# Batches 14 and 15 of a transformer layer: the second normalisation in two ScalarE passes, and a new order of the last units

## The reference

```python
x = L0_attn_x                                            # [16, 256, 256] float32
x = x + attn(_layernorm(x), wq, wk, wv, wo)              # 16 heads, 4 KV heads, head size 128
x = x + ffn(_layernorm(x), weight, bias)

# attn: softmax(q k^T / sqrt(128)) v, then wo; a query sees the first 4 keys and the last 32
# ffn:
x_scale = max(max(abs(x), axis=2) / 127, 1e-12)          # one per row
x_q = clip(round(x / x_scale), -128, 127)
y = (x_q @ w_q.T) * x_scale * w_scale + bias             # w_q, w_scale: weight quantised by row
```

## Time and profile before

| | |
|---|---|
| median of three runs | 606.9 us (606.56 to 607.15) |
| the profiled execution: its time | 609.35 us |
| its span, first to last instruction | 607.5 us |
| busy: TensorE, weight load, VectorE, ScalarE, POOL | 593.1, 524.7, 537.0, 397.6, 313.7 us |
| mean granted matmul clock | 0.99 |

### The profile page before, as it was taken

One profiled execution on the slowest core, in us unless ns is written; L12 is line 12 of the kernel. 1 busy time (PEld: TensorE's weight loads), 2 busy tenths in 40 slices (PEclk: granted clock), 3 DMA queues, 4 the chain that ended last, 5 costly groups with the idle time before them and its releaser, 6 DMA issues.

```text
span 607.5 us, 18044 instructions
## 1 busy us (share of the span) xinstructions
PE 593.1 (98%) x7556; PEld 524.7 (86%) x7556; DVE 537.0 (88%) x1073; ACT 397.6 (65%) x625; POOL 313.7 (52%) x310
## 2 busy tenths in 40 slices
PE   7999999999999999999999999999999999999994
PEld 6779888898988989898898988889898898989983
DVE  6999999898989979899898889889898997989996
ACT  6898665676666667666666666567666666765660
POOL 2155364555647455564645646455564745546472
PEclk8999999999999999999999999999999999999998
DMA  8748042150604216060340605115060311506001
GB/s 298 237 93 190 3 107 53 61 115 19 158 19 95 63 38 139 19 149 10 85 92 28 148 19 119 41 61 116 20 139 19 94 48 38 121 19 139 2 19 35
DMA packets 36272, 49.69 MB, mean 82 GB/s; under 512 B 2784, under 2 KB 22240, under 8 KB 36192
## 3 DMA queue, kind: packets, MB, share of 16 engines
q1 hardware_dynamic: 36048, 48.41, 32.1%
q10 hardware_dynamic: 144, 0.13, 0.1%
HBM read 35.42 MB, written 12.58 MB: 79 GB/s over the span
## 4 chain that ended last, share of the span: by engine, by line
PE 88%; DVE 4%; POOL 3%; issue 2%; ACT 2%; DMA 1%; SPq 0%; DVEq 0%; POOLq 0%
PE ps L414 25%; PE ps L536 25%; PE ps L445 8%; PE ps L382 7%; PE ps L393 6%; PE ps L489 5%; PE ps L519 4%; PE ps L518 4%; DMA small<-in_L_attn_wv 1%; PE ps L370 1%; PE ps L582 1%; POOL Sm L1433 1%; POOL small L1444 1%; DVE sm L1051 1%; POOL PP L1450 1%
## 5 line engine op out<-in xcount | busy, mean ns | idle before, releaser
L414 PE MATMUL ps<-xT,WqT 128*128 128x256 f16 x1536 | 180.7, 274 | 1.0 <-DVE Qs L1033 0.7
L536 PE MATMUL ps<-WoT,pool 128*128 128x256 f16 x1440 | 167.2, 273 | 0.1
L414 PEld LDWEIGHTS ps<-xT,WqT 128*128 128x128 f16 x1536 | 147.8, 98 | 18.2 <-DVE Qs L1033 1.0
L536 PEld LDWEIGHTS ps<-WoT,pool 128*128 128x128 f16 x1440 | 138.3, 98 | 15.5 <-DVE pool L1060 0.3
L1444 POOL TENSOR_TENSOR small<-E,rr 128x576 f32<-128x576 f32 x64 | 73.7, 1152 | 108.2 <-DVE rr L1055 108.0
L861 ACT ACTIVATE pool<-ps 128x512 f16<-128x512 f32 x128 | 70.0, 594 | 81.5 <-PE ps L519 81.5
L812 ACT ACTIVATE Qs<-ps 128x576 f16<-128x576 f32 x128 | 82.8, 647 | 41.8 <-PE ps L414 41.8
L1450 POOL TENSOR_TENSOR PP<-small,PP 128x576 f16<-128x576 f32 x64 | 82.0, 1282 | 52.5 <-ACT PP L848 52.5
L1033 DVE TENSOR_TENSOR Qs<-ps,Qs 128x576 f16<-128x576 f32 x128 | 92.7, 727 | 3.2 <-ACT Qs L812 3.2
L1433 POOL TENSOR_TENSOR Sm<-Sm,mx 128x576 f32<-128x576 f32 x64 | 73.7, 1152 | 37.3 <-DVE mx L1046 36.0
L1060 DVE SCALAR_TENSOR_TENSOR pool<-ps,pool 128x512 f16<-128x512 f32 x128 | 82.1, 679 | 0.1
(11 more groups left out here) (125 smaller groups left out, 890.3 us busy)
## 6 DMA issues: line engine op xcount, KB each, us to landing
values<-Vn SPq DMA_DIRECT2D x32, 256.0 KB, 2.0
VW<-values SPq DMA_DIRECT2D x16, 480.0 KB
big<-values SPq DMA_DIRECT2D x16, 480.0 KB
X<-in_L_attn_x SPq DMA_DIRECT2D x16, 256.0 KB, 8.5
VW<-values SPq DMA_DIRECT2D x16, 240.0 KB
big<-values SPq DMA_DIRECT2D x16, 240.0 KB
out<-pool SPq DMA_DIRECT2D x15, 256.0 KB, 5.9
big<-in_L_attn_wq SPq DMA_DIRECT2D x4, 512.0 KB, 9.2
```

Of the source, the lines that this page charges most:

```text
L414: a = pe.matmul(banks[BANK_Q[f]][:, j * 256:j * 256 + 256], WqT[:, k, wl, h * 128:h * 128 + 128], xT[:, b % 2, k, xl, :], start=(n == 1), ...
L536: a = pe.matmul(out_view(b, t), OT[:, p, ol, h, t * 128:t * 128 + 128], WoT[:, 4 * g + h, wl, :], start=first, stop=(end and g == KV - 1), ...
```

## The change

It does two things.

Batches 14 and 15 are normalised by ScalarE in two passes instead of by one VectorE instruction per half. The first pass writes mean - x (`ffn_centre`, `last_centre`: Identity with scale -1 and the mean as bias) and needs no rstd. The second multiplies by rstd (`ffn_scaled`, `last_scaled`). The values have their sign turned. VectorE takes the peak from the first pass (magnitudes have no sign) and multiplies it by rstd in an instruction of its own on one or two columns; the scale is made negative (times -1/127, and a minimum with -1e-12), so that the reciprocal turns the sign back. The scale in the product is then negative, so the last additions became subtractions. VectorE's scaling reads ScalarE's second output in place. POOL's `last_rstd` waits for ScalarE's two scaling passes of batch 14.

The order of the last units is written anew on all engines: scores, halves of `pv` and `out_last` are split and interleaved differently on TensorE; both last transposes stand ahead of the last matmuls; the sum of a half follows its product at once; `o_low` calls stand between the steps of batch 14's quantisation.

```diff
@@ TensorE
             q_fill(NU - 2, 0)
+            pv(NU - 5, 0)
             scores(NU - 3)
+            pv(NU - 5, 1)
             q_fill(NU - 2, 1)
-            pv(NU - 5, 0)
             ffn_t(B - 3)
-            pv(NU - 5, 1)
+            p_transpose(NU - 4)
             q_fill(NU - 1, 0)
-            p_transpose(NU - 4)
             scores(NU - 2)
             q_fill(NU - 1, 1)
+            out_proj(NU - 5, (0,))
             pv(NU - 4, 0)
             pv(NU - 4, 1)
-            out_proj(NU - 5, (0, 1))
+            out_proj(NU - 5, (1,))
             scores(NU - 1)
+            ffn_mm(B - 3)
             p_transpose(NU - 3)
             out_proj(NU - 5, (2, 3))
             pv(NU - 3, 0)
-            ffn_mm(B - 3)
             pv(NU - 3, 1)
             out_last(0, 1, (0, 1))
-            out_last(0, 0, (0, 1))
+            out_last(0, 0)
             p_transpose(NU - 2)
-            out_last(0, 0, (2, 3))
             out_last(0, 1, (2, 3))
+            out_last(1, 0, (0, 1))
             pv(NU - 2, 0)
+            out_last(1, 1, (0, 1))
             pv(NU - 2, 1)
-            out_last(1, 0)
+            out_last(1, 0, (2, 3))
             p_transpose(NU - 1)
-            out_last(1, 1)
+            out_last(2, 0, (0, 1))
+            out_last(1, 1, (2, 3))
             pv(NU - 1, 0)
             pv(NU - 1, 1)
-            out_last(2, 0)
+            out_last(2, 1, (0, 1))
+            out_last(2, 0, (2, 3))
             out_last(3, 0)
-            out_last(2, 1)
+            out_last(2, 1, (2, 3))
             out_last(3, 1)
             ffn_t(B - 2)
             ffn_mm(B - 2)
             ffn_last_t(0)
+            ffn_last_t(1)
             ffn_last_mm(0)
-            ffn_last_t(1)
             ffn_last_mm(1)
@@ ScalarE, new functions
+            def ffn_centre():
+                act.wait_ge(f_st, 4 * (B - 1))
+                for t in range(2):
+                    act.activation(xn2[:, t, :], X[:, 2 * (B - 2) + t, :], ACT.Identity, bias=mv2[:, t, 0:1], scale=-1.0).then_inc(f_d, 1)
+            def ffn_scaled():
+                act.wait_ge(f_rs, 2 * (B - 1))
+                act.wait_ge(f_d, 2)
+                for t in range(2):
+                    act.activation(xr[:, t, :], xn2[:, t, :], ACT.Copy, scale=rs2[:, t, 0:1]).then_inc(f_n, 1)
...
@@ ScalarE, start of the tail's order
+            q_high(NU - 2, 0)
             p_high(NU - 4)
-            q_high(NU - 2, 0)
+            o_high(NU - 5, 0)
+            o_high(NU - 5, 1)
             q_high(NU - 2, 1)
-            o_high(NU - 5, 0)
+            ffn_t_evac(B - 3)
             exps(NU - 3)
-            ffn_t_evac(B - 3)
-            o_high(NU - 5, 1)
+            q_high(NU - 1, 0)
             pt_evac(NU - 4)
-            q_high(NU - 1, 0)
+            q_high(NU - 1, 1)
             p_high(NU - 3)
-            q_high(NU - 1, 1)
             o_high(NU - 4, 0)
@@ VectorE, new functions
+            def ffn_turned_peak():
+                dve.wait_ge(f_d, 2)
+                dve.tensor_reduce(fx[B % 2][:, 0:2], xn2[:, :, :], AX.X, ALU.max, apply_absolute_value=True).then_inc(f_s, 1)
+            def ffn_turned_steps():
...
+                dve.tensor_tensor(f[:, 0:2], f[:, 0:2], rs2[:, :, 0], ALU.mult).then_inc(f_s, 1)
+                dve.tensor_scalar(f[:, 2:4], f[:, 0:2], -1.0 / 127.0, -1e-12, ALU.mult, ALU.min).then_inc(f_s, 1)
+                dve.reciprocal(f[:, 4:6], f[:, 2:4]).then_inc(f_s, 1)
...
-                dve.tensor_tensor(yo[:, (B - 1) % 2, t, :], yo[:, (B - 1) % 2, t, :], xr[:, t, :], ALU.add).then_inc(f_z, 1)
+                dve.tensor_tensor(yo[:, (B - 1) % 2, t, :], yo[:, (B - 1) % 2, t, :], xr[:, t, :], ALU.subtract).then_inc(f_z, 1)
@@ VectorE, start of the tail's order
+            q_low(NU - 2, 0)
             s_mask(NU - 3)
             s_peak(NU - 3)
-            q_low(NU - 2, 0)
+            o_low(NU - 5, 0)
             q_low(NU - 2, 1)
-            o_low(NU - 5, 0)
+            o_low(NU - 5, 1)
             probs(NU - 3)
-            o_low(NU - 5, 1)
@@ POOL
+                pool.wait_ge(f_n, 2)
                 pool.tensor_tensor(rs2[:, t:t + 1, 1], mv2[:, t:t + 1, 1], cst[:, 0:1], ALU.add).then_inc(f_rs, 1)
...
+            residual_bias(B - 3)
             p_low(NU - 4)
             s_shift(NU - 3)
-            residual_bias(B - 3)
```

More of the change, by code:

```diff
@@ L167, in build @@
                                             sem("p_n"), sem("p_l"))
+        f_d, f_n, f_pk = sem("f_d"), sem("f_n"), sem("f_pk")
         f_rs, f_o, f_xb = sem("f_rs"), sem("f_o"), sem("f_xb")
@@ L841, in ffn_last_t_evac, with last_centre, last_scaled @@
                 act.activation(xqT[:, :, t * 128:t * 128 + 128], xq_view(B - 1, t), ACT.Copy).then_inc(f_t, 1)
+            def ffn_centre():
[7 more added lines that the diff above has]
+                    act.activation(xr[:, t, :], xn2[:, t, :], ACT.Copy, scale=rs2[:, t, 0:1]).then_inc(f_n, 1)
+            def last_centre(t):
+                act.wait_ge(f_st, 4 * (B - 1) + 2 * t + 2)
+                act.wait_ge(f_n, 2)
+                act.activation(xn2[:, t, :], X[:, 2 * (B - 1) + t, :], ACT.Identity, bias=mv2[:, t, 0:1], scale=-1.0).then_inc(f_d, 1)
+            def last_scaled(t):
+                act.wait_ge(f_rs, 2 * (B + t))
+                act.wait_ge(f_d, 3 + t)
+                act.wait_ge(f_xq, B - 1)
+                act.activation(xr[:, t, :], xn2[:, t, :], ACT.Copy, scale=rs2[:, t, 0:1]).then_inc(f_n, 1)
             def p_high(u):
@@ L990, in _ @@
             o_high(NU - 2, 1)
+            ffn_centre()
             pt_evac(NU - 1)
             o_high(NU - 1, 0)
+            ffn_scaled()
             o_high(NU - 1, 1)
+            last_centre(0)
+            last_scaled(0)
             ffn_t_evac(B - 2)
+            last_centre(1)
+            last_scaled(1)
             ffn_last_t_evac(0)
@@ new lines, in ffn_turned_scale, with last_peak @@
+            def ffn_turned_scale():
+                dve.wait_ge(f_s, 3 * (B - 2) + 4)
+                dve.wait_ge(f_n, 2)
+                for t in range(2):
+                    dve.tensor_scalar(xr[:, t, :], xr[:, t, :], fx[B % 2][:, 4 + t:5 + t], MAGIC, ALU.mult, ALU.add).then_inc(f_xr, 1)
+            def last_peak(t):
+                dve.wait_ge(f_d, 3 + t)
+                dve.tensor_reduce(fx[(B - 1) % 2][:, t:t + 1], xn2[:, t, :], AX.X, ALU.max, apply_absolute_value=True).then_inc(f_pk, 1)
@@ L1132, in last_peak, with last_step @@
+            def last_step(t):
+                f, n = fx[(B - 1) % 2], 3 * (B - 2) + 4 + 3 * t
+                dve.wait_ge(f_pk, t + 1)
+                dve.wait_ge(f_rs, 2 * (B + t))
+                dve.tensor_tensor(f[:, t:t + 1], f[:, t:t + 1], rs2[:, t:t + 1, 0], ALU.mult).then_inc(f_s, 1)
                 dve.wait_ge(f_s, n + 1)
-                dve.tensor_scalar(f[:, 2 + t:3 + t], f[:, t:t + 1], 1.0 / 127.0, 1e-12, ALU.mult, ALU.max).then_inc(f_s, 1)
+                dve.tensor_scalar(f[:, 2 + t:3 + t], f[:, t:t + 1], -1.0 / 127.0, -1e-12, ALU.mult, ALU.min).then_inc(f_s, 1)
@@ L1380, in _ @@
             ffn_out(B - 3)
+            o_low(NU - 3, 1)
             ffn_stats(B - 2)
-            o_low(NU - 3, 1)
             o_low(NU - 2, 0)
+            ffn_turned_peak()
             o_low(NU - 2, 1)
-            ffn_norm(B - 2)
-            ffn_peak(B - 2)
+            ffn_turned_steps()
             o_low(NU - 1, 0)
+            ffn_turned_scale()
+            ffn_round(B - 2)
             o_low(NU - 1, 1)
-            ffn_scale(B - 2)
-            ffn_round(B - 2)
             last_residual(0)
             last_stats(0)
-            last_norm(0)
+            last_peak(0)
             last_residual(1)
             last_stats(1)
-            last_peak(0)
+            last_step(0)
+            last_peak(1)
             last_scale(0)
-            last_norm(1)
-            last_peak(1)
+            last_step(1)
             last_round(0)
@@ L1404, in _ @@
             last_product(0)
+            last_sum(0)
             last_product(1)
-            last_sum(0)
             last_sum(1)
```

20 lines of the change are left out of this document (10 added, 10 removed).

## The result

| | before | the change |
|---|---|---|
| first comparison: median (range, executions) | 606.9 us (606.56 to 609.33, 22) | 605.88 us (604.81 to 608.66, 22) |
| ratio, 95% interval | | 0.9981 (0.9973 to 0.9990) |
| second comparison: median | 607.1 us | 605.24 us (604.92 to 606.11, 5) |
| ratio, 95% interval | | 0.9967 (0.9955 to 0.9980) |
| profiled execution: span | 607.5 us | 605.1 us |

A forecast was written before the change was run, and what follows sets the result against it. TensorE was taken as 98% busy, the gain lying in its waits and VectorE's last chain. t = 1's residual 1.4 us sooner plus 0.7 after it gave -2.1, from 606.9 to 604.8 us; range 604.1 to 606.3.

The forecast's parts named there:

- a hole that stays: Rival, chance 0.15: o_low(63, 0) ends up to 1 us late, so TensorE still waits before the last projections; 605.8 us.
- a lost wait at a transpose: Upper end of the range: a transpose wait of 0.4 us, added to the hole before the last projections, gives 606.3.
- Early part costs nothing: 567 to 579 us: same instructions in another order, TensorE has no wait, cost nothing, with 0.4 us to spare in one place.
- the three transposes' waits go: TensorE's waits for POOL's p_low at three transposes vanish: -0.43 us, with 0.2 to 0.3 us to spare at two.
- ScalarE's pass 0.51: Each of the eight added 256-column passes on ScalarE was taken to last 0.51 us.
- The hole of 1.26 closes with nothing to spare: TensorE's 1.26 us wait for VectorE's o_low before the last projections vanishes; batch 14's transposes come 1.5 us sooner, t = 1's residual 1.4.
- The small step behind the multiply: On VectorE in batch 14's quantisation: a small tensor_scalar starting under POOL's bias is held to its end, to 591.65.
- From the residual to the last sum 7.0 us instead of 7.70: Kernel's end, t = 1's residual to last sum: 7.0 us instead of 7.70, with the first sum held under POOL's addition.
- Stores 0.7 sooner: Kernel's end: batch 14's store and ScalarE's store are issued 0.7 us sooner, counted from t = 1's residual.
- The free sum: Rival, chance 0.20: the first last sum is not held by POOL, ScalarE's store comes 0.7 us sooner; 604.5 us.
- The stores bind: Rival, chance 0.08: three last stores issued within 0.5 us instead of 1.2 queue up: +0.3, 605.1 us.
- The slower rival: Rival, chance 0.07: about six ScalarE passes lie on the path; gain gone at 0.86 us each, 1.2 us slower at 1.06.

The follow-up runs named there:

- w0: Kernel before plus nine constant matmuls in TensorE's start-up gaps: median 607.04 us, 39.86 us from the first matmuls of q_fill(62, 0) to the span's end.
- w1: The changed kernel plus nine constant matmuls in TensorE's start-up gaps: median 605.35 us, 37.97 us from the first matmuls of q_fill(62, 0) to the span's end.
- e1: Kernel before with only the new order of calls on all engines, normalisation left on VectorE: median 607.49 us, ratio 1.0000.
- r1: The changed kernel run again unaltered, for a second profile and more times: median 605.24 us.
- e3: The changed kernel with the second product moved ahead of the first sum, so both products precede both sums: median 605.2 us.
- p2: The changed kernel plus nine start-up matmuls, with all eight ScalarE passes run twice, the extra ones into a spare buffer: median 607.1 us.
- e2: Kernel before with only ScalarE's two sign-turned passes, order of calls as before on all engines: median 605.39 us, ratio 0.9968.

## Why the prediction was right, and where it was not

The forecast was 604.8 with a range from 604.1 to 606.3, the first median 605.88. The sum spoke of -2.1 us between two kernels in the same condition; the tail shows -1.97, w0 and w1 show -1.7 in the median. So the mechanism and its size came out, and the median, which fell by 1.0, did not. Two terms were missing in the step from the profile to the median. The start: the front of this document already showed it, in an execution of 609.35 beside a median of 606.9, and the prediction took its distance to the median for granted. And what a time has beyond its span, taken as 1.85 throughout, which is 2.16 to 2.36 in twelve of the change's 22 executions. They make about 0.6 and 0.4 of the 1.1 us between forecast and median. That 605.88 lies in the range is in part luck: its upper side was set for a hole that stays and a lost wait at a transpose, and neither happened.

- *Early part costs nothing, the three transposes' waits go.* Right in the trace: no such wait is left. But e1 shows that by themselves they are worth nothing, because VectorE's chain sets the end. The prediction counted their 0.43 us through TensorE's path alone.
- *ScalarE's pass 0.51.* Measured 0.51 alone, and 0.40 more for one that follows another. The prediction came to 0.51 from other operations' rows. The Trainium skill, page "ScalarE: Activation LUTs", section "What ACT_TABLE_LOAD costs", has about 280 ns + 0.833 ns per column with a pointer operand and an overlap of 93 ns back to back; an estimate from that page's figures is 0.49 and 0.40 for 256 columns, and the rows agree.
- *The hole of 1.26 closes with nothing to spare.* Right but for 0.2 that is left of it. -1.36 at the transposes against -1.5, and -1.25 at t = 1's residual (28.64 against 29.89 us into the tail) against -1.4.
- *The small step behind the multiply is held to POOL's end.* The place was right, the instruction wrong: the multiply itself started under POOL and was held, 1.08. I had let it run free in 0.15. It cost the same, since both end with POOL's bias. This was a slip against the rule that the prediction cites two paragraphs further down: the multiply has two inputs from SBUF.
- *From the residual to the last sum 7.0 us instead of 7.70.* 602.87 - 595.88 = 6.99. The sum was held, 0.97 (1.26 in r1), and ended 6.14 us after the residual, forecast 6.15.
- *Stores 0.7 sooner.* Batch 14's was issued 601.77 - 595.88 = 5.89 after the residual; forecast 5.9. From there to the end 3.33, before 3.36.
- *The free sum would give 0.3 more (0.20).* This rival failed in its price: e3 brings ScalarE's store 0.51 us forward and nothing moves. The wrong step was that a sooner store of ScalarE, the last to be issued, would move the end. The end hangs on the start of the stream, SP's store of batch 14. *The stores bind* named the right place and a wrong price: closer issues add nothing (3.36 us from the first one to the end before, 3.33 now), since the stream is full in both.
- *The slower rival: six passes count.* 5.3 by p2. All eight run twice take the whole gain of the tail and 0.2 more; at 5.3 passes the 1.89 of the tail are gone with 0.36 more for each, a pass of 0.87, where the prediction said 0.86.

Left open: what exactly decides in the first 20 us whether the clock falls, and what the 0.4 to 0.5 us are that some executions with the passes take beyond their span. A version with passes for batch 14 alone was not tried, so the 1.74 of e2 is not split between the hole and the last quantisation.

## What to carry to other kernels

Take an instruction off the engine whose chain of dependences sets the end, not the one that is busiest: TensorE was 98% busy, and still a new order on it alone gave nothing, while taking two instructions per batch off VectorE gave 1.7 us, though it put eight passes on ScalarE (66% busy), about five of which count on the path. While the last stores form one full stream, the issue of the first of them sets the end, and issuing the later ones sooner gains nothing: send the big block off in pieces as they become ready. And when a gain of 0.3% is measured, compare a stretch that starts at a fixed instruction, make the start of the kernel repeatable, and set spans beside times before reading medians.
